# Block numbers packed once a pair, so that eight of them lie side by side when an engine loads them into registers

## What is computed

```python
h = jnp.maximum(_layernorm(x, axis=-1), 0.0)
x = x + _L0_gnn_ref(h, ...)      # mids = f(y[edge_src], edge attributes, a small MLP on 8 scalars)
                                 # agg = segment_sum(mids, edge_dst); then linear maps
h = jnp.maximum(_layernorm(x, axis=-1), 0.0)
# _L1_gnn_ref: two attention layers, each
#   h = x @ W;  e = leaky_relu(a_s[src] + a_d[dst]);  alpha = softmax of e over the edges of one dst
#   out = segment_sum(h[src] * alpha, dst)
x = x + _L1_gnn_ref(h, edge_index, ...)
```

## Time and profile before

| what | us |
|---|---|
| median of 3 runs (lowest to highest) | 4856.83 (4851.91 to 4860.45) |
| span of the profiled execution, first to last instruction | 4836.3 |
| busy in it: PE, DVE, POOL, ACT | 3107.3, 3044.1, 2895.1, 2574.7 |
| register loads: DVE 174, PE 116, SP 464 | not counted as busy |

### The profile page before, as it was taken

How to read it: one execution, slowest core, us unless ns; L and a number is a source line. 1 busy time by engine, 2 the same in 40 slices (tenths; PEclk the granted TensorE clock), 3 DMA queues, 4 the chain that set the end, 5 groups by cost and what they waited for, 6 DMA issues and landing times. The chain is left out here.

```text
span 4836.3 us, 56702 instructions
## 1 busy us (share of the span) xinstructions
PE 3107.3 (64%) x11125; PEld 1876.3 (39%) x11125; DVE 3044.1 (63%) x8069; ACT 2574.7 (53%) x7729; POOL 2895.1 (60%) x2918
## 2 busy tenths in 40 slices
PE   4699999989998883455555555555354555555451
PEld 3344444444444372333333334433233333333331
DVE  7788888878887753455555455566354555555557
ACT  3598888888888642333334334344243334343347
POOL 2366666656665405677777767733676777777763
PEclk8899999999999996677777767778576777767776
DMA  5233323333322244444444444424444444444445
GB/s 165 93 88 87 86 86 86 87 85 86 87 85 84 72 127 134 112 129 118 129 123 124 129 118 129 131 61 127 117 126 121 122 125 128 118 129 124 124 108 161
DMA packets 274567, 540.54 MB, mean 112 GB/s; under 512 B 73156, under 2 KB 161983, under 8 KB 274240
## 3 DMA queue, kind: packets, MB, share of 16 engines
q0 software_dynamic: 134912, 376.36, 28.8%
q1 hardware_dynamic: 132308, 154.29, 10.3%
q10 hardware_dynamic: 7020, 6.40, 0.4%
HBM read 495.47 MB, written 41.31 MB: 111 GB/s over the span
## 5 line engine op out<-in xcount | busy, mean ns | idle before, releaser
L1247 POOL DMA_INDIRECT arena<-h_rows,idx x1856 | 1893.8, 1020 | 972.0 <-issue 515.2
L1382 PE MATMUL ps<-arena,z 128*128 128x264 f32 x3712 | 1328.7, 511 | 493.1 <-DVE arena L1494 290.8
L769 POOL DMA_INDIRECT arena<-y_rows,idx x928 | 901.0, 971 | 717.7 <-ACT arena L800 359.1
L1306 ACT ACTIVATE z<-z 128x256 f32<-128x256 f32 x928 | 382.2, 412 | 1504.0 <-remote 833.3
L1382 PEld LDWEIGHTS ps<-arena,z 128*128 128x128 f32 x3712 | 856.6, 249 | 728.2 <-DVE arena L1494 351.7
L1502 DVE TENSOR_TENSOR z<-ps,z 128x264 f32 x928 | 396.1, 427 | 1105.3 <-remote 713.3
L798 ACT ACTIVATE arena<-arena 128x128 f32<-128x128 f32 x2784 | 912.0, 393 | 110.8 <-DVE arena L885 64.4
L840 PE MATMUL ps<-arena 128*128 128x512 f32 x1856 | 902.5, 610 | 4.6 <-DVE z L893 4.6
L1298 ACT ACTIVATE z<-iota,dst_x 128x128 f32<-128x128 f32 x1856 | 644.5, 395 | 26.4
L1494 DVE TENSOR_TENSOR arena<-arena,z 128x520 f32<-128x520 f32 x928 | 639.0, 689 | 1.8 <-ACT z L1287 1.1
L832 PE MATMUL ps<-arena 128*128 128x512 f32 x928 | 495.6, 617 | 121.2 <-DVE arena L885 85.2
(11 more groups left out here) (231 smaller groups left out, 2838.3 us busy)
## 6 DMA issues: line engine op xcount, KB each, us to landing
z<-lo_rows SPq DMA_DIRECT2D x116, 512.0 KB
arena<-h_rows,idx POOLq DMA_INDIRECT x1856
arena<-y_rows,idx POOLq DMA_INDIRECT x928
z<-seg_rows SPq DMA_DIRECT2D x232, 64.0 KB
h_rows<-arena SPq DMA_DIRECT2D x98, 132.0 KB, 1.8
arena<-h_rows SPq DMA_DIRECT2D x98, 132.0 KB, 3.0
arena<-res_rows SPq DMA_DIRECT2D x98, 128.0 KB, 3.0
z<-in_ea_rows SPq DMA_DIRECT2D x464, 8.0 KB
```

Source lines behind the costliest of these rows:

```text
L769: pool.indirect_dma_start(out=ring[:, r, :], out_offset=None, in_=s.y_rows, in_offset=bass.IndirectOffsetOnAxis(ap=rows_of[:, u, n:n + 1], ...
L1247: pool.indirect_dma_start(out=ring[:, u * SCORED + n, :], out_offset=None, in_=h_rows, in_offset=bass.IndirectOffsetOnAxis(ap=s.idx[:, u, ...
L1306: nc.scalar.activation(sel[:, q % SELS, :, :].rearrange("p k n -> p (k n)"), away[:, q % 2, :, :].rearrange("p k n -> p (k n)"), ACT.Relu, ...
L1382: last = t.matmul(ps[:, bank[q % 4], 0:ROW], sel[:, q % SELS, k, :], ring[:, u * SCORED + 2 * q + k, :], start=(k == 0), stop=(k == 1))
```

## The change

`s.blk` gets half the columns and one number for each pair. The DMA that fills it takes every second word of `block_line`. Both kinds of load address it by pair, and the load of eight reads words that are next to each other instead of two apart. The number of loads, the words loaded by each, and every wait stay as they are.

```diff
@@ -72,7 +72,7 @@ (blocks_of_pairs)
-                s.blk[0:1, 2 * first:2 * first + 16:2], engines=(engine,), min_val=0, max_val=BLOCKS - 1,
+                s.blk[0:1, first:first + 8], engines=(engine,), min_val=0, max_val=BLOCKS - 1,
@@ -181,7 +181,7 @@ (build)
-        s.blk = sb("blk", [1, SLOT_COLS], I32)
+        s.blk = sb("blk", [1, SLOT_COLS // 2], I32)
@@ -336,7 +336,8 @@ (prepare)
-                sp.dma_start(s.blk[:, :], s.block_line.rearrange("n o -> o n")).then_inc(got_blk, 16)
+                with nc.allow_non_contiguous_dma(reason="512 words, once"):
+                    sp.dma_start(s.blk[:, :], s.block_line.rearrange("(n k) o -> k (n o)", k=2)[0:1, :]).then_inc(got_blk, 16)
@@ -749,7 +750,7 @@ (conv_edges)
-                block = sp.value_load(s.blk[0:1, 2 * pair:2 * pair + 1], min_val=max(0, pair - PAIRS + 1), max_val=min(pair, BLOCKS - 1))
+                block = sp.value_load(s.blk[0:1, pair:pair + 1], min_val=max(0, pair - PAIRS + 1), max_val=min(pair, BLOCKS - 1))
```

## The result

The changed kernel takes 4898.61 us (median of 4 runs, 4896.90 to 4901.30), the kernel before, run beside it, 4854.46 (4 runs, 4851.91 to 4860.45): 1.010 times the time, with a 95% interval of 1.0086 to 1.0113. It is 44 us slower. The forecast was 4858 us in a range of 4770 to 4868, and its main rival was a gain.

A forecast was written before the change was run, and what follows sets the result against it. It took PE, closely followed by ACT and DVE, to pace conv_edges and POOL's gathers the attention layers. Loads 0, SP and tile 0, DMA +1 us on 4836.3 gave 4837, plus 20.5 made 4858 us; range 4770 to 4868.

The forecast's parts named there:

- main rival: Loads on DVE and PE: neighbouring words come in one read, 92 us less, 4765 us; chance 0.29.
- first rival: Same as the main rival: cheap loads give 28 us in conv_edges plus 64 us in the attention layers; chance 0.29.
- The load's price: Loads of eight on DVE and PE: still 1832 and 1927 ns when words are neighbours, so 0 us gained.
- The fit of 45 + 223 ns a word: Register loads: a fixed 45 ns plus 223 ns for each word, from SP's 268 ns and DVE's 1832 ns.
- The estimate of 491 ns for two reads: Load of eight, if its words came in two reads of 16 bytes: 45 + 2 x 223 = 491 ns.
- The gap before the add closes: DVE before L893 in conv_edges: any load under 0.85 us removes 0.98 us idle each, at most 55.1 us in the stretch.
- Half of it is a gain (28 us), half comes back as a wait in L879: DVE in conv_edges: of at most 57 us idle time, 28 us is gained, as PE sets the pace.
- The attention layers give 64 us: Both attention layers: half of DVE's at most 128 us saved counts, where POOL waits for the ring, 264 us.
- SP's load, the tile's size: SP's one-word loads and blk being 2 KB a partition shorter, moving later tiles: 0 us each.
- The DMA of 512 words: Filling blk in preparation with single 4-byte words instead of one 4 KB row: +1 us, ends 0 and +10 us.
- The rival on the slower side: Preparation: the DMA of 512 words stops other engines, 5 to 10 us, 4866 us; chance 0.06.
- The time outside the span, 20.5 us: Whole kernel: median of runs lies 20.5 us above the profiled span of 4836.3 us, carried over unchanged.

The follow-up runs named there:

- the backward load: Changed kernel with DVE's load of eight in conv_edges read from last word to first: 0.9996 of before on B, 1.0015 on C, 0.9997 on E.
- E: A chip: kernel before 4862.55 us; changed kernel 4907.26 us, and with DVE's conv_edges load read last word to first 4860.35 us.
- B: A chip: kernel before 4391.86 us; ran variants with reversed load, doubled load, every other gather left out, and POOL pauses.
- half-gathers run: Changed kernel with every other gather of conv_edges left out, the even slot's rows used for both: 1.0002 of before on B, 0.9641 on D.
- D: A chip: kernel before 4850.10 us; changed kernel 4890.30 us, 1.0077.
- A: A chip: kernel before 4856.18 us; packed numbers for DVE in conv_edges alone 1.0091, in the attention layers alone 0.9997.
- pauses put in directly: Two small memsets with waits on POOL before every eighth conv_edges gather: changed kernel 0.9997 on B, 0.9928 on C; kernel before 1.0025 on D.
- C: A chip: kernel before 4833.70 us; changed kernel 4827.35 us, 1.0000.
- six slots: Changed kernel with POOL allowed six slots ahead instead of eight in conv_edges: 1.0098 of before on C.

## Why the prediction was wrong, step by step

The forecast of no change rests on one step, the price of a load, and that step failed. It doesn't explain the sign, though: with the right price the prediction's own sum is that of its first rival, a gain of 92 us. What failed in that rival is the conversion of shorter waits into time, 28 us and 64 us.

- **The load's price: wrong, and the first step that failed.** "I take the upper one" of 1832 and 268 ns, because distance seemed to cost nothing. Measured: 597 ns on DVE, 591 on PE. The fit of 45 + 223 ns a word was right only for words that are not one behind the other upwards: the backward load still takes 1831. The Trainium skill's rule ("Runtime: NRT & Kernel Launch", section "Instruction fetch mechanics") of about 200 ns a register "even for bulk", which the page has for loads from HBM, doesn't carry over to these: eight registers took 597 ns. The estimate of 491 ns for two reads was near, and too low.
- **The gap before the add closes: right** for the rival that had short loads, 55.1 us to 0.1.
- **Half of it is a gain (28 us), half comes back as a wait in L879: wrong, by size and by sign, and the step on which the slowdown hangs.** All came back and 35 us more, and `conv_edges` got longer (by 67 us in E's two profiles, 47 in the medians of the runs). On B and in the half-gathers run, where nothing is held, the trade is nearly exact: gap and wait together are 55.2 + 23.1 = 78.3 us with the long load on B, and 0.1 + 75.3 = 75.4 with the short one in the half-gathers run on D, in the same length of stretch. PE's pace is the bound there, and the gap was free. The text had PE's 119.8 us of idle time as DVE's doing; on D it is gone entirely when half the gathers are left out, with the short load and the same DVE work, so it needs the gathers; DVE's pace alone doesn't make it.
- **The attention layers give 64 us: wrong, 0.** The run with packed numbers there alone is at 0.9997. POOL's ring waits looked like what the loads would shorten, but more than 124 of this layer's 152.9 us end in a "remote". On B a layer takes 1211 us from first gather to last with no such wait (19.8 us on ring room in all). That is 23 us under the 1234 that the prediction took for the least: a gather and its issue take 1.00 + 0.30 us there, not 1.33. Held updates are my reading of the difference there too; no run with fewer gathers in these layers was made.
- **SP's load, the tile's size: right,** 265 ns, and the run with the old size as slow as the changed one.
- **The DMA of 512 words: right that it is small.** The first gather starts at 167.8 us against 165.9; over all profiles of either kind it is 165.8 to 169.5, so +1 us can't be told, and +10 us did not come. The rival on the slower side named this mechanism and was wrong about it.
- **The time outside the span, 20.5 us: mis-sized.** It compared one profile with the median of other runs. In the changed kernel's profiled execution, time and span are 4901.3 and 4899.2: 2.1 us. By that the profiled execution of before took 4838.4 us, under the fastest of its runs (4851.91), which fits its being from another chip.
- **What was missing** is a rival in which an engine that stops waiting changes when another issues. The long "remote" waits, 156.6 us in the earlier trace rows, were not asked about: they are six tenths of the idle time in these two rows and end at no instruction's end.

**What is shown and what isn't.** Shown: the loss lies in `conv_edges`, on A, and comes from the shorter hold of DVE's sequencer there, on E; and PE's late completions, with the idle time of PE behind them, vanish on D when half the gathers do. Argued only: that DVE's 1 us gap works by making ACT late, so that ring room comes later and POOL's run of gathers ends sooner. The run lengths fit, but pauses put in directly gave 0.9928 on C with the short load and 1.0025 on D with the long one, and six slots made it slower. So pauses alone don't make the time; that the order in which gathers and matmuls fall does is my reading. Open: what holds the updates, why B never does, why C loses nothing, and why fewer bursts cost more. Every run has its span and clock from the profiler, so none shows whether the recording itself has a part in the late updates or in the difference between chips. No run pairs the short load with pauses on A, D or E. No version was found that beats both kernels on all chips.

## What to carry to other kernels

A register load of eight neighbouring words in rising order costs a third of the same words at any other order tried here; but look first whether the engine that loads is ever waited for: where its gap and the wait that stands next on it only trade places, as on B, the gap is free. If large waits end in a "remote" rather than at an instruction's end, shortening another wait can change the rhythm of gathers against matmuls and lose time, so such a change needs runs on several chips, and kernels are compared only within one. Where gathers run beside a PE-bound stage, fewer gathers can be worth more than shorter waits: leaving out half of them gave 3.6% here on one chip, and nothing on another.

## What the runs showed of the hardware that was not expected

- Eight words side by side: 597 ns (DVE), 591 (PE); the same eight read backwards 1831 (DVE), eight at a distance of two 1832 (DVE) and 1927 (PE).
- The same program takes 4392 us on one chip and 4834 to 4863 on four others. The difference lies in the stages with gathers: from first to last gather `conv_edges` takes 1306 us against 1478 to 1546 (without pauses and with all gathers), a layer 1211 against 1336 to 1355.
- On the four chips the traces show none of PE's semaphore updates for up to 12 us while gathers follow each other, and then a burst. They also lack events: in 204 to 1440 us there are 4.0 landing events for each gather of the stage before and 3.4 changed, where B has 16.0 and D with half the gathers 15.3; and 717 of PE's 846 updates changed, where B has 993 of 994. So a single "remote" may also be a missing event, and a wait is to be read from the engines' own rows.
- The Trainium skill ("DMA: Bandwidth & Descriptors", section "SWDGE vs HWDGE vs iDMA") says that for a DMA issued by GpSimd a core of it computes the descriptors and writes them into rings in SBUF, unlike one issued by SP. The 0.95 us that POOL spends on each gather agree with work of that kind; no run shows that it is these writes that hold the updates.
